# Diagonal score blocks of four heads in one PSUM bank, seeded with the causal mask by ScalarE: an attention and mixture-of-experts kernel on one Trainium2 core

## What is computed

```python
scores = jnp.einsum('bhtd,bhsd->bhts', q, k) * scale
causal = jnp.triu(jnp.ones((T, T), dtype=bool), 1)
scores = jnp.where(causal, -jnp.inf, scores)
attn = jax.nn.softmax(scores, axis=-1)
seq_out = jnp.einsum('bhts,bhsd->bhtd', attn, v)
```

## Time and profile before

| | |
|---|---|
| three runs | 1018.55, 1021.79, 1023.22 us; median 1021.79 |
| the profiled execution | 1023.56 us; span from first to last instruction 1021.9 us |
| TensorE busy | 922.9 us, 90% of the span; granted clock 0.961 on average |
| VectorE, ScalarE, GpSimd busy | 736.5, 595.0, 425.8 us |
| attention steps 1 to 8 (by the row maxima's copies) | 51.6 to about 585 us |

### The profile page before, as it was taken

How to read it: one execution, slowest core, us unless ns; L and a number is a source line. 1 busy time by engine, 2 the same in 40 slices (tenths; PEclk the granted TensorE clock), 3 DMA queues, 4 the chain that set the end, 5 groups by cost and what they waited for, 6 DMA issues and landing times. The chain is left out here.

```text
span 1021.9 us, 26568 instructions
## 1 busy us (share of the span) xinstructions
PE 922.9 (90%) x7976; PEld 672.6 (66%) x7977; DVE 736.5 (72%) x2689; ACT 595.0 (58%) x1357; POOL 425.8 (42%) x389
## 2 busy tenths in 40 slices
PE   4688999998899999999997989999999999999960
PEld 1244666656556666576564678888889978888850
DVE  4727789897787898989987677775655676555564
ACT  3246465564463555645555578676577756666663
POOL 6417144464183544644445534332222253233333
PEclk9789999999899999999999999999999999999985
DMA  4875203304114123041040543233223233233265
GB/s 147 259 203 141 64 23 95 96 22 141 51 53 137 43 89 102 1 137 53 22 146 2 184 163 82 51 48 49 43 43 71 47 85 53 42 52 52 39 191 180
DMA packets 60086, 89.48 MB, mean 88 GB/s; under 512 B 8636, under 2 KB 49488, under 8 KB 58928
## 3 DMA queue, kind: packets, MB, share of 16 engines
q1 hardware_dynamic: 44952, 61.80, 20.7%
q0 software_dynamic: 13728, 21.90, 11.3%
q10 hardware_dynamic: 1280, 4.19, 1.1%
HBM read 52.26 MB, written 35.47 MB: 86 GB/s over the span
## 5 line engine op out<-in xcount | busy, mean ns | idle before, releaser
L2007 DVE CUSTOM_DVE_ANT_0 junk<-sm,mask_ts 128x512 bf16<-128x512 f32 (+3 forms) x512 | 219.6, 486 | 59.4 <-PE sm L1405 58.0
L1145 ACT ACTIVATE arena_b<-st 128x512 f32<-128x512 f32 x320 | 180.2, 598 | 112.1 <-PE st L1367 111.0
L987 POOL DMA_INDIRECT sums<-arena_b x64 | 112.6, 1759 | 253.3 <-DVE arena_b L2241 243.3
L2203 DVE TENSOR_TENSOR arena_b<-arena_b 128x256 f16<-128x256 f32 (+1 forms) x280 | 116.1, 428 | 96.3 <-ACT arena_b L1221 93.9
L1365 PE MATMUL st<-arena_a 128*128 128x384 f16 (+3 forms) x512 | 127.0, 305 | 13.2 <-DMA arena_a<-max_row 7.5
L1405 PE MATMUL sm<-arena_a 128*128 128x512 f16 (+3 forms) x512 | 113.9, 310 | 12.8 <-DVE maxes L2007 6.5
L1556 PE MATMUL st<-arena_b,arena_a 128*128 128x256 f16 (+1 forms) x840 | 112.3, 271 | 6.4 <-DVE arena_b L1887 4.9
L1569 PE MATMUL pv<-arena_a,arena_b 128*128 x816 | 112.3, 274 | 0.0
L1556 PE MATMUL sm<-arena_b,arena_a 128*128 128x256 f16 (+1 forms) x840 | 110.7, 268 | 0.0
L1569 PE MATMUL sm<-arena_a,arena_b 128*128 x792 | 109.4, 274 | 0.0
L1217 ACT ACTIVATE arena_b<-sm,arena_b 128x256 f32<-128x256 f32 (+1 forms) x140 | 65.5, 468 | 65.8 <-PE sm L1556 50.6
(11 more groups left out here) (364 smaller groups left out, 1740.3 us busy)
## 6 DMA issues: line engine op xcount, KB each, us to landing
arena_b<-slots SPq DMA_DIRECT2D x32, 260.0 KB, 2.7
arena_a<-w SPq DMA_DIRECT2D x8, 1024.0 KB, 6.0
arena_b<-x_tr SPq DMA_DIRECT2D x8, 512.0 KB, 4.0
q_rows<-arena_b SPq DMA_DIRECT2D x32, 128.0 KB
k_rows<-arena_b SPq DMA_DIRECT2D x32, 128.0 KB
arena_a<-q_rows SPq DMA_DIRECT2D x32, 128.0 KB
arena_a<-k_rows SPq DMA_DIRECT2D x32, 128.0 KB
res<-x_tok POOLq DMA_DIRECT2D x8, 512.0 KB, 4.3
```

Of the source, the lines that this page charges most:

```text
L987: pool.indirect_dma_start(sums, bass.IndirectOffsetOnAxis(ap=token_now[:, 1 - par, m:m + 1], axis=0), y_out[1 - par][:, m, :], None, compu ...
L1145: act.activation(probs[:, q, :], st_ps[piece % 2][:, :], ACT.Exp, scale=SCORE_SCALE).then_inc(exp_done, 1)
L2007: last = dve.tensor_tensor_reduce(junk[:, n % 3, at:at + width], sm_ps[n % 3][:, at:at + width], mask_ts[:, T - width:T], 1.0, NEG, ALU.ad ...
L2203: dve.tensor_tensor(g_lo[par][:, hc, 0:rows], g_32[:, hc % 4, 0:rows], g_hi[par][:, hc, 0:rows], ALU.subtract).then_inc(hid_done, 1)
```

## The change

Scores are now made in 44 pieces per batch, eleven for each group of four heads, of two kinds. *Diagonal* pieces (numbers 0, 7, 8 and 10 of a group) hold the diagonal 128 columns of the same key block s of all four heads, four matmuls of 128 columns. The other pieces hold what lies beside the diagonal: 384 columns of one head (1 to 4), 256 of two heads (5, 6), 128 of four heads (9). No mask is multiplied; instead, when ScalarE has finished the exponential of piece p and piece p+2, which uses the same bank, is diagonal, it waits for its own exponential and then copies the mask triangle four times into the bank, and the diagonal matmuls add to it. TensorE waits for that copy (`mask_put`) before a diagonal piece. Only piece 0 of the first step, with no piece before it, still uses four mask matmuls. The exponential writes the same slots of `probs` through a view. The second half of the maxima rows is now awaited by piece 22, and the list of stages is in another order.

```diff
-        ("late_maxima", 0), ("scores", 0), ("late_maxima", 1), ("o_tokens", 0), ("scores", 1), ("scores", 2), ("o_tokens", 1),
+        ("scores", 0), ("late_maxima", 0), ("scores", 1), ("late_maxima", 1), ("o_tokens", 0), ("scores", 2), ("scores", 3),
...
+        def pieces_of(piece):
+            g, k = piece // 11, piece % 11
+            heads = range(4 * g, 4 * g + 4)
+            if k in (0, 7, 8, 10):
+                s = {0: 0, 7: 1, 8: 3, 10: 2}[k]
+                return "diagonal", [(h, s, s, P * (h % 4)) for h in heads]
+            if k < 5:
+                return "rest", [(heads[k - 1], 0, 1, 0)]
+            if k < 7:
+                return "rest", [(h, 1, 2, 2 * P * (h % 2)) for h in heads[2 * k - 10:2 * k - 8]]
+            return "rest", [(h, 2, 3, P * (h % 4)) for h in heads]
...
                 def exps(piece):
-                    act.activation(probs[:, q, :], st_ps[piece % 2][:, :], ACT.Exp, scale=SCORE_SCALE).then_inc(exp_done, 1)
+                    bank, to = st_ps[piece % 2], slots_of(piece)
+                    m, width = to.shape[1], to.shape[2]
+                    act.activation(to, bank[:, 0:m * width].rearrange("p (m t) -> p m t", m=m), ACT.Exp, scale=SCORE_SCALE).then_inc(exp_done, 1)
+                    if pieces_of((piece + 2) % 44)[0] == "diagonal" and (piece + 2 < 44 or before_end(i, 0)):
+                        act.wait_ge(exp_done, n_of(44 * b + piece + 1))
+                        act.activation(bank[:, :].rearrange("p (m t) -> p m t", m=4), mask_st[:, :].unsqueeze(1).broadcast_to([P, 4, P]), ACT.Copy).then_inc(mask_put, 1)
...
                 def scores(piece):
+                    kind, blocks = pieces_of(piece)
+                    seeded = kind == "diagonal" and (piece > 0 or later(i, 2))
-                    if piece >= 2 or later(i, 2):
-                        pe.wait_ge(exp_done, n_of(40 * b + piece - 1))
+                    if seeded:
+                        pe.wait_ge(mask_put, n_of(masks_put(b, piece)))
+                    elif piece >= 2 or later(i, 2):
+                        pe.wait_ge(exp_done, n_of(44 * b + piece - 1))
+                    for m, (h, s, first, at) in enumerate(blocks):
+                        width = width_of(piece, s, first)
+                        last = pe.matmul(out[:, at:at + width], ks[:, h % 2, h // 2, s * P:(s + 1) * P], qs[:, h // 2, first * P:first * P + width],
+                                         start=m == 0 and not seeded, stop=kind == "rest" or seeded, skip_group_check=True)
```

More of the change, by code:

```diff
@@ L70, in stages_of_a_step @@
-        ("late_maxima", 15), ("projection", 1), ("projection", 2), ("projection", 3), ("values", 2), ("layernorm", 0), ("layernorm", 1),
-        ("scores", 14), ("turn", 3), ("late_maxima", 16), ("late_maxima", 17), ("queries", 0), ("seed", 0), ("scores", 15),
-        ("scores", 16), ("late_maxima", 18), ("late_maxima", 19), ("queries", 1), ("scores", 17), ("layernorm", 2), ("norms", 0),
-        ("late_maxima_rows", 0), ("queries", 2), ("layernorm", 3), ("maxima", 0), ("queries", 3), ("load_w2", 0), ("scores", 18),
@@ new lines, in stages_of_a_step @@
+        ("queries", 0), ("seed", 0), ("late_maxima", 18), ("scores", 17), ("scores", 18), ("late_maxima", 19), ("queries", 1),
+        ("scores", 19), ("layernorm", 2), ("norms", 0), ("values", 3), ("late_maxima_rows", 0), ("queries", 2), ("layernorm", 3),
+        ("maxima", 0), ("scores", 20), ("queries", 3), ("load_w2", 0), ("scores", 21), ("maxima", 1), ("maxima", 2),
+        ("first_weights", 0), ("scores", 22), ("scores", 23), ("scores", 24), ("maxima", 3), ("values", 4), ("normalise", 0),
@@ new lines, in stages_of_a_step @@
+        ("scores", 32), ("scores", 33), ("maxima", 14), ("memory", 0), ("memory", 1), ("first_weights", 3), ("maxima", 15),
+        ("scores", 34), ("scores", 35), ("tables", 0), ("maxima", 16), ("scores", 36), ("values", 7), ("maxima", 17), ("rank", 0),
+        ("first_expert", 0), ("maxima", 18), ("scores", 37), ("memory", 2), ("maxima", 19), ("values", 8), ("scores", 38),
+        ("scores", 39), ("memory", 3), ("memory", 4), ("scores", 40), ("scores", 41), ("maxima_rows", 0), ("memory", 5),
@@ L84, in stages_of_a_step @@
+        ("first_rows", 0), ("scores", 42), ("values", 9), ("scores", 43), ("values", 10), ("values", 11),
     ]
@@ L570, in attention_and_ffn, with width_of, masks_put, slots_of @@
         maxima_blocks = (((0, 3, 0),), ((1, 3, 0),), ((0, 2, 0), (0, 0, 3 * P)), ((1, 2, 0), (1, 0, 3 * P)), ((0, 1, 0), (1, 1, 2 * P)))
+        def pieces_of(piece):
[9 more added lines that the diff above has]
+            return "rest", [(h, 2, 3, P * (h % 4)) for h in heads]
+        def width_of(piece, s, first):
+            return P if pieces_of(piece)[0] == "diagonal" else T - first * P
+        def masks_put(b, piece):
+            return 16 * b + 4 * (piece // 11) + {0: 0, 7: 1, 8: 2, 10: 3}[piece % 11]
+        def slots_of(piece):
+            kind, blocks = pieces_of(piece)
+            h, s, first, _ = blocks[0]
+            at = (first - s) * P
+            width = width_of(piece, s, first)
+            hl = h % 4
+            if s == 0:
+                return probs[:, hl:hl + len(blocks), at:at + width]
+            if s == 2:
+                return probs[:, 8:10, :].rearrange("p a (m t) -> p (a m) t", m=2)[:, hl:hl + len(blocks), at:at + width]
+            at += 3 * P if s == 3 else 0
+            return probs[:, 4 + hl:4 + hl + len(blocks), at:at + width]
         def later(i, n):
@@ L777, in before_late @@
                 sp.wait_ge(table_done, 9)
-            sp.wait_ge(st_ready, 40 * B)
+            sp.wait_ge(st_ready, 44 * B)
             load_weights(2)
```

67 lines of the change are left out of this document (28 added, 39 removed).

## The result

The changed kernel takes 1042.5 us (median of 4 runs, 1040.5 to 1044.0) against 1022.3 for the kernel before (4 runs): ratio 1.0199, 95% interval 1.0175 to 1.0224, 20 us slower. Forecast were 1031 us and a range up to 1042. The profiled execution took 1043.2 us with a span of 1041.5 and a mean granted clock of 0.951 (before 0.961). A few executions fell into a much slower state (one each of e1, e2, e5 and, beside e1 to e4, of before); the times given here leave these out.

What follows compares the result with a forecast made beforehand. TensorE, busy for 90% of 1021.9 us, was taken as the bound. Seven steps gave +7.5 us, the loop's turn -1.2, the last step +2.7: about +9 on the median 1021.8, so 1031 us, range 1011 to 1042.

Steps and rivals of the forecast that it cites:

- Removed: Sixteen 512-column matmuls leave TensorE per step: 3.45 us saved per step, 27.6 us in eight, if nothing else moved.
- Added on ScalarE: Sixteen mask fills per step, taken as 0.60 us each, 0.63 of queue: 10.1 us per step, which ScalarE has.
- B: Rival: no change, as fills cost about 0.3 to 0.4 us and waits equal the saving; 1024 us, chance 0.24.
- C: Rival: clearly slower, as a fill costs 1 us; 1049 us, chance 0.06.
- Where TensorE now waits: Five numbered places in a steady step: 4.5 us of new waits against 3.45 saved, about +1.1 us per step.
- place 1: End of the step: the maxima row copy comes later, so piece 0 of the next step waits; +1.18 us.
- place 4: Pieces 22 to 24: 22 waits for the maxima row, 24 for its exponential; +0.6 us.
- place 5: Piece 36 behind 34, +0.4 us; behind these, later ScalarE copies of projected lines and tokens, and piece 14, +0.8 us.
- The last steps: Seventh step counted as steady, +1.1 us; last step 6.2 us of new waits less 3.45 saved, +2.7 us.
- Rival D: Longer waits drop TensorE's clock: 2 us a step at most, 1047; expected once or twice, 1033 to 1035; no chance given.
- the tail is untouched: The part of the kernel after the attention was taken as unchanged, with nothing for it in the sum.
- Rival A: Faster: fills stay hidden behind other TensorE work, deciding at 3.45 us of new waits per step; about 1011 us, chance 0.20.

Runs made afterwards that it cites:

- e1: The changed kernel without its fills and without any causal mask on the scores: 1015.6 us, ratio 0.995 to the kernel before.
- e2: The changed kernel with each diagonal bank's masks put in by one 512-column matmul on TensorE instead of a ScalarE fill: 1030.9 us, ratio 1.009 to before.
- e5: The changed kernel with the fill behind piece 41 moved behind ScalarE's copy of the maxima row: 1033.7 us, ratio 1.013 to before.
- e4: The kernel before with its 64 mask matmuls per step left out and nothing in their place: 1011.6 us, ratio 0.992 to before.
- e6: The changed kernel with zero-weight matmuls put where TensorE waits, before pieces 8, 24, 30 and, in the last two steps, 22: 1035.4 us, ratio 1.014 to before.
- e12: The kernel before with 5 zero-weight matmuls ahead of piece 20 in its last two steps: 1022.9 us, ratio 1.003 to before.
- e8: e5 with one mask matmul instead of the fill at pieces 8 and 30 and at all diagonal pieces of the last two steps: 1024.1 us, ratio 1.003.
- e10: e2 with the stage list of the kernel before, the 44 pieces laid in by columns: 1034.8 us, ratio 1.016 to before.
- e11: The changed kernel with as many zero-weight matmuls as e6, all before piece 14, where TensorE doesn't wait: 1058.3 us, ratio 1.039 to before.

## Why the prediction was wrong

*Removed.* 3.45 us a step was to be TensorE's own time; in the fifth step of e4 its busy time falls by 2.95 us (64.61 to 61.66). As a saving it was about three times too large when nothing else changed: 9.3 us in all instead of 27.6, 1.4 in a full-clock step; and with the new pieces (e1) 5. The text said that VectorE would give part of it back, and put nothing for it in the sum.

*Added on ScalarE.* Right: 601 ns, 0.63 apart, 77 us. Rivals B and C fall with it. B stood beside a statement of the Trainium skill, "ScalarE: Activation LUTs", section "Step-by-step: what each stage is for", that writing to PSUM is the faster way out of ScalarE. This trace shows no gain at 512 columns: 601 ns for the copy from SBUF to PSUM, 597 for the exponential from PSUM to SBUF. As the two also read from different places, no run tells what the write alone costs.

*Where TensorE now waits.* All five places wait, and by their names. The forecast counted from where the next matmul could have started, and idle time in the rows begins later, when the last one is through the array: 0.17 us, by the prediction's estimate. With these 0.17 added, the sixth step has +0.4 at place 1 (0.81 idle, 0.38 before; +1.18 forecast), 0.64 at piece 8 (+0.65), 1.03 at piece 30 (+0.9), 0.56 and 0.33 at place 4 (+0.6), 0.37 at piece 36 (+0.4). Their sum is 3.4; the further +0.8 of place 5 shows only in the values' wait (0.45). That is 3.4 to 3.8 instead of 4.5, and the saving was too large as well. In the rows of the sixth step TensorE's busy time falls by 2.5 us (64.54 to 62.02), where 3.45 were to go, and its idle time grows by 3.1 (1.26 to 4.38). So the net of +1.1 came out (+1.0, +1.0, +0.6) partly by luck. The third step alone differs by 1.2 us between two traces of the same instructions, so that these are no sharp confirmation.

*The last steps.* The seventh was counted as steady, though it has no queries either. It has the waits that the forecast kept for the last step: pieces 18 and 19 wait 0.89 and 0.71 us for fills, piece 22 waits 1.71 for its maxima row, 0.50 before. With half as much half-clock time (e6: 3.4 us instead of 6.8) it is +2.7 over before, not +1.1; the eighth, with 3.4 us at half clock as before the change, is -0.3, not +2.7. (The parts of the 3.8 us for places 1, 2, 4 and 5 in the last step add to 3.6; nothing hangs on it.)

*The step that failed* is the price of the clock. Rival D gave it "2 us a step at most", "once or twice", and the sum of +9 had nothing for it. Measured are 17 us more at half clock in the attention (30.6 against 13.6), in three steps 6.8, 6.8 and 10.2 us where before had 0, 0 and 3.4; that is up to 3.4 us in each. Over all runs up to 10 us more are lost (49.2 against 39.0), and fillers in the waits win back 7. If the waits had cost the forecast's 9, with 7 to 10 from the clock the sum is 16 to 19 of the 20 us. The step beside it that failed is the seventh, counted as steady: its waits are worth about 1 us more (+5.8, less up to 3.4 of clock, less the 1.1 forecast). The rest is not settled: part of it may be the 3.9 us behind the attention. That part of the profiled executions varies from 436.1 to 444.4 us over all 14 kernels here, with the same instructions; in the five that had 6.8 us at half clock there, ahead of the kernel's end, it was 436.1 to 438.8, but e12 with 10.2 had 436.5 and the changed kernel with as much 440.0. So "the tail is untouched" held for the work; its time was not mine to promise, and what moves it is open.

*Rival A* set its point at 3.45 us of new waits per step. The waits came to about that, and still a step was 0.6 to 1.0 us longer, since TensorE's busy time fell by 2.5 and not 3.45. Even with no fills, part of the saving comes back as waits: e4's fifth step has 2.95 us less of busy time and 1.4 less of time. That fills can be hidden where other work lies between, as it said, shows in e8, with 14 of the 16 fills in its steady steps: 65.1 and 64.8 us in the fifth and sixth, 66.2 and 65.8 before.

## What to carry to other kernels

Price removed work by what a kernel without it does, not by the engine's busy time: here a step had 1.4 us to win of 3.45, and moving the work put its price (a bank that comes back 0.63 us later) on the path at five places out of sixteen. Ask what each new wait does to TensorE's clock: here the half-clock time that came with waits of 0.4 to 3 us took 7 to 10 us beside the waits themselves. And count the pieces: the same columns cut into 44 instead of 40 cost 14 us in an unchanged order. That a rotation of two banks pays per return is my reading of it; e10 shows the longer waits for exponentials, but it also has four weight loads in a row per diagonal piece, and no run parts the two.

## What was not expected of the hardware

- Work put into TensorE's waits made the kernel faster (e6: 16 us of matmuls more, 7 us less time), while the same work elsewhere cost its full 15.8 us (e11).
- Taking work off TensorE can lower its clock: e4 did 27.6 us less, and over ten runs 48.4 us were lost to the clock against 39.0. How much stands at half clock varies too, though: before, e2, e10 and e12 have nearly the same columns on TensorE, and 13.6, 17.0, 6.8 and 10.2 us in their profiled executions.
- The same wait of piece 30 stands in steps 2 to 7 of the changed kernel (0.84 to 0.86 us idle). In steps 5 and 7 a fall of the clock stands within 3 us behind it, in the other four none does. In a stretch of the same length with nearly the same busy time no fall follows (below, beside 2.56 above), and before's fall at 569.2 us has no wait ahead. What brings one on, busy time and waits alone do not tell.

```profile
440.90:444.30 3.40, 2.54 (x29) 1.85 (x26) 2.57 (x11) 3.37 (x9) 3.22 (x3) 1.00 0.73 212
```
